# Reciprocals of attention's column sums moved from ScalarE to VectorE, in a transformer layer on eight cores

## The reference, cut to what matters

```python
# x: (8, 2048, 1024) float32; 16 heads of 64
def attn(x, W_qkv, W_out):
    qkv = einsum('bsd,ndh->bnsh', x, W_qkv)
    q, k, v = split(qkv, 3, axis=-1)
    a = einsum('bnqh,bnkh->bnqk', q, k) / sqrt(64)
    a = softmax(a + causal_mask, axis=-1)
    out = einsum('bnqk,bnkh->bnqh', a, v)
    out = out.reshape(B, -1, S)                      # (8, 1024, 2048)
    return einsum('bds,nhd->bsd', out, W_out)        # out[b,d,s] * sum over n,h of W_out[n,h,d]

x = x + attn(layernorm(x), W_qkv, W_out)
x = x + (relu(layernorm(x) @ w1 + b1) @ w2 + b2)     # 1024 -> 4096 -> 1024
```

## Time and profile before

| what | value |
|---|---|
| median of 3 runs | 1007.05 us (1004.82 to 1007.62) |
| the profiled execution's own time | 1006.95 us |
| its span on the slowest core (core 1) | 1005.2 us |
| spans of the eight cores | 998.5 to 1005.2 us |
| PE busy | 913.5 us, 91% of the span |
| DVE busy | 426.4 us, 42% |
| ACT busy | 388.2 us, 39% |
| POOL busy | 68.0 us, 7% |

### The profile page before, as it was taken

One profiled execution on the slowest core, in us unless ns is written; L12 is line 12 of the kernel. 1 busy time (PEld: TensorE's weight loads), 2 busy tenths in 40 slices (PEclk: granted clock), 3 DMA queues, 4 the chain that ended last, 5 costly groups with the idle time before them and its releaser, 6 DMA issues.

```text
span 1005.2 us, 12813 instructions; the slowest of 8 cores (998.5 to 1005.2 us)
## 1 busy us (share of the span) xinstructions
PE 913.5 (91%) x4624; PEld 381.0 (38%) x4624; DVE 426.4 (42%) x612; ACT 388.2 (39%) x505; POOL 68.0 (7%) x54
## 2 busy tenths in 40 slices
PE   3768999998999999999672999999999999999998
PEld 1323433333333333333221444444444444444443
DVE  4662035545454646363537662037310752124301
ACT  2223369797979787888881010001000010000000
POOL 1310010101010000000003030003000020000000
PEclk9788999999999999999895999999999999999999
DMA  9930259896978000010604242023410332024111
GB/s 212 257 58 0 43 91 109 99 117 79 115 76 113 2 1 1 1 43 1 209 16 153 101 150 105 32 74 126 168 41 33 136 126 105 34 71 162 48 42 42
DMA packets 27804, 85.31 MB, mean 85 GB/s; under 512 B 2272, under 2 KB 10464, under 8 KB 22880
## 3 DMA queue, kind: packets, MB, share of 16 engines
q0 software_dynamic: 15504, 25.76, 20.1%
q1 hardware_dynamic: 12240, 58.74, 16.6%
HBM read 101.34 MB, written 25.17 MB: 126 GB/s over the span
## 4 chain that ended last, share of the span: by engine, by line
PE 81%; ACT 6%; DVE 4%; DVEq 3%; issue 3%; DMA 2%; ACTq 1%; SPq 0%
PE arena L422 22%; PE arena L444 22%; PE arena L345 11%; PE arena L308 9%; PE arena L325 8%; PE arena L287 5%; ACT p_sb L520 4%; PE arena L334 2%; DMA x_sb<-x 2%; DVEq L549 2%; PE arenab L268 1%; DVE osc_sb L569 1%; ACT lnf_sb L466 1%; DVE t_sb L585 1%; ACTq L511 1%
## 5 line engine op out<-in xcount | busy, mean ns | idle before, releaser
L520 ACT ACTIVATE p_sb<-arena 128x1024 bf16<-128x1024 f32 (+1 forms) x320 | 273.4, 895 | 43.3 <-PE arena L334 26.1
L422 PE MATMUL arena<-lnf_sb,wstage 128*128 128x512 bf16 x1024 | 226.4, 382 | 1.4 <-ACT lnf_sb L466 1.4
L345 PE MATMUL arena<-p_sb,v_all 128*128 128x512 bf16 (+3 forms) x640 | 172.9, 352 | 14.2 <-DVE osc_sb L569 14.1
L422 PEld LDWEIGHTS arena<-lnf_sb,wstage 128*128 128x128 bf16 x1024 | 100.2, 98 | 121.5 <-issue 5.2
L308 PE MATMUL arena<-lnf_sb,wstage 128*128 128x512 bf16 x448 | 138.0, 380 | 0.0
L645 DVE TENSOR_SCALAR h_sb<-arena,b1c_sb 128x512 bf16<-128x512 f32 x128 | 94.9, 747 | 95.6 <-PE arena L422 95.6
L325 PE MATMUL arena<-qpair,kpair 64*128 64x512 bf16 (+3 forms) x640 | 115.3, 355 | 14.4 <-ACT p_sb L520 14.3
L444 PE MATMUL arena<-w2hi_sb,h_sb 128*128 128x512 bf16 x512 | 115.7, 379 | 0.0
L444 PE MATMUL arena<-lnf_sb,h_sb 128*128 128x512 bf16 x512 | 115.7, 379 | 0.0
L660 DVE TENSOR_TENSOR x_sb<-arena,x_sb 128x512 f32<-128x512 f32 x32 | 22.1, 692 | 198.6 <-PE arena L444 198.6
L454 ACT ACTIVATE rsd_sb<-bag_sb,cst_sb 128x2 f32<-128x2 f32 (+1 forms) x12 | 3.6, 298 | 219.2 <-DVE bag_sb L543 219.1
(11 more groups left out here) (39 smaller groups left out, 428.7 us busy)
## 6 DMA issues: line engine op xcount, KB each, us to landing
wstage<-w1b SPq DMA_DIRECT2D x32, 1024.0 KB, 4.8
x_sb<-x SPq DMA_DIRECT2D x16, 512.0 KB, 22.3
w1b<-w POOLq DMA_DIRECT2D x8, 1024.0 KB, 32.1
w2b<-w POOLq DMA_DIRECT2D x8, 1024.0 KB, 38.7
y<-x_sb SPq DMA_DIRECT2D x32, 256.0 KB, 2.0
lnf_sb<-w2b SPq DMA_DIRECT2D x2, 2048.0 KB, 16.3
w2hi_sb<-w2b SPq DMA_DIRECT2D x2, 2048.0 KB, 12.8
wstage<-wqk POOLq DMA_DIRECT2D x7, 512.0 KB, 7.9
```

What stands on the lines that cost most here:

```text
L345: mm = e.matmul(AP(arena, (4 + h) * 512 + off, [[AR, 128], [1, w]]), v_all[:, j, pair, 64 * h:64 * h + 128], AP(p_sb, (n % 3) * 1024 + h * ...
L422: mm = e.matmul(bankap(ww % 4, TF), AP(wstage, 4 * ((n // 4) % 2) * 1024 + dc * 512 + (ww % 4) * 128, [[8 * 1024, 128], [1, 128]]), lnf2_s ...
L520: e.activation(AP(p_sb, (n % 3) * 1024, [[3 * 1024, 128], [512, 2], [1, w]]), AP(arena, 2 * (n % 2) * 512 + off, [[AR, 128], [512, 2], [1, ...
```

## The change: what it does

ACT's `reciprocal` and its semaphore `act_rec` go. `o_finish` on DVE, at the same place in DVE's order, no longer waits for a semaphore. It first drains, then transposes the sums within blocks of 32 x 32 into `rec_sb`, 64 partitions for each head with the same crossing of the halves. All rows of a block of sums are equal, so after the transpose each column of a block holds its 32 different sums, and column 0 of each of the 16 blocks is enough: a new tile `r16_sb` of 128 x 16 takes the reciprocals of these 16 columns. It is multiplied by WB's 16 columns in place, and a third transpose, which reads each of the 16 columns 32 times, writes `rec_sb` in the layout of before. The four products, the sum and everything else are unchanged.

```diff
@@ tiles and semaphores
         rec_sb = asb("rec_sb", [128, 512], F32)
+        r16_sb = asb("r16_sb", [128, 16], F32)
-        act_p, act_rec = sem("act_p"), sem("act_rec")
+        act_p = sem("act_p")
@@ scalar (ACT)
-            def reciprocal(ep):
-                e.wait_ge(dve_oc, 2 * ep + 2)
-                if ep >= 1:
-                    e.wait_ge(dve_t, ep)
-                e.activation(rec_sb[0:64, :], osc_sb[64:128, ep % 2, 0:512], AF.Ln)
-                e.activation(rec_sb[64:128, :], osc_sb[0:64, ep % 2, 512:1024], AF.Ln)
-                e.drain()
-                e.activation(rec_sb[:, :], rec_sb[:, :], AF.Exp, scale=-1.0).then_inc(act_rec)
-
-            ep = 0
...
-                if n >= 3 and is_last(n - 3):
-                    reciprocal(ep)
-                    ep += 1
-            reciprocal(ep)
@@ vector (DVE), o_finish
-                e.wait_ge(act_rec, ep + 1)
+                e.drain()
+                e.transpose(rec_sb[0:64, :], osc_sb[64:128, ep % 2, 0:512])
+                e.transpose(rec_sb[64:128, :], osc_sb[0:64, ep % 2, 512:1024])
+                e.drain()
+                e.reciprocal(r16_sb[:, :], AP(rec_sb, 0, [[512, 128], [32, 16]]))
+                e.drain()
                 e.tensor_mul(
-                    AP(rec_sb, 0, [[512, 128], [32, 16], [1, 32]]),
-                    AP(rec_sb, 0, [[512, 128], [32, 16], [1, 32]]),
-                    AP(WBp_sb, pair * HD + 16 * qb, [[NPAIR * HD, 128], [1, 16], [0, 32]]))
+                    r16_sb[:, :], r16_sb[:, :],
+                    AP(WBp_sb, pair * HD + 16 * qb, [[NPAIR * HD, 128], [1, 16]]))
+                e.drain()
+                e.transpose(rec_sb[:, :], AP(r16_sb, 0, [[16, 128], [1, 16], [0, 32]]))
                 e.drain()
```

## The result

The changed kernel takes 1024.48 us at the median against 1007.34 us of the kernel before; the ratio is 1.0173, with a 95% interval from 1.0150 to 1.0195. The forecast was 1022 us, and slower. The profiled execution took 1025.08 us.

A forecast was written before the change was run, and what follows sets the result against it. PE (TensorE, 81% of the chain) was taken as the bound, stalled once a pair by VectorE's late copy; +10.9 + 8.1 - 1.0 - 2.9 - 0.1 = +15.0 us on 1006.95 gives 1022 us, range 1010 to 1034.

The forecast's parts named there:

- Work added on VectorE: In o_finish, transposes, small operations and drains ahead of the products: 2.81 us where 0.77 us stood before.
- P: Time from the start of o_finish's first instruction to its t_sb products: 0.77 us before, 2.81 us forecast, ends 1.97 and 4.64.
- the lower end of 0.41 us: Lower bound for one 512-column fp32 transpose, half of a one-source operation's 0.81 us on 1024 columns.
- rivals 3 and 4: Quick transposes (P = 1.97), 1007 to 1015 us, chance 0.11; ScalarE's relief wins (P under 1.59), 1003 us, chance 0.06.
- The stall: PE's wait for the copy at the end of block 0 grows from 1.36 to 3.17 us; six pairs, +10.9 us.
- The clock: After each of six 3.17 us PE stalls the granted clock falls, costing 1.35 us each: +8.1 us.
- Rival 1: Late copies at block 0, but the clock kept: +6.9 us, 1013.9 us, chance 0.13.
- ScalarE in pairs 1 to 6: PE's wait of 0.17 us after each of the six block 0 boundaries, following a reciprocal, goes: -1.0 us.
- ScalarE in pair 7: PE's waits of 1.34 us at blocks 1 to 2 and 2 to 3 go, exponentials start 1.46 us earlier: -2.9 us.
- Pair 7's first stall: Pair 6's finish reaches its products at 482.67 instead of 482.78: -0.1 us; the 3.81 us stall and slow clock stay.
- The tail: At the end of attention, the last products start at 528.60 against 528.61: nothing.

The follow-up runs named there:

- e5: Kernel before, with 1.83 us of unused added work on VectorE in the finish of query block 3 only; 1024.5 and 1028.3 us, ratio 1.0191.
- e6: Kernel before, with the same 1.83 us of added VectorE work in the finishes of blocks 0, 1 and 2 only; 1009.5 us.
- e3: Changed kernel with twelve extra matmuls, their sums overwritten, in each of six places where PE waits for the late copy; 1015.0 us, ratio 1.0077.
- e10: Changed kernel with every output copy ahead of the competing finish on VectorE (finishes after steps 3, 11, 23, 27); 987.0 us, ratio 0.9803.
- e11: Kernel before, reciprocals on ScalarE with two buffers, all copies first (finishes after steps 3, 11, 23, 27); 990.96 us, ratio 0.9842.
- e7: Changed kernel with transposes, reciprocal and WB product moved to right behind the output copy, ahead of the next eviction; 1010.23 us, ratio 1.0034.
- e4: Changed kernel with the copy ahead of the finish at the end of block 0 only; 1038.33 us, ratio 1.0303.
- e2: Kernel before, copies ahead of finishes at blocks 0 and 1, later finishes moved, two reciprocal buffers; 991.37 us, ratio 0.9844.

## Why the prediction was right, step by step

Measured between the profiled executions on core 1, where the end of the last copy's wait moved by 543.01 - 524.34 = 18.67 us.

- *Work added on VectorE.* P was put at 2.81 us and is 2.86: transposes 0.71 us each for 0.69 taken, the small operations 0.25 and 0.17 for 0.21 each. That a one-source operation on fp32 ran at twice the rate in the earlier trace rows said nothing of the transpose, so the lower end of 0.41 us, on which rivals 3 and 4 rested, was not there. The Vector Engine (DVE) Microarchitecture Reference of the Trainium skill, section 3.8, has one element per cycle per lane. The 0.71 us agree with it, as they lie above the 0.53 us that the prediction estimated from that page.
- *The stall.* Forecast 3.17 us and +10.9 us. Measured 3.18 to 3.22 us, together 19.15 against 8.17: +11.0 us. e5 and e6 show that nearly all of the loss comes from the finishes of block 3.
- *The clock.* Forecast +8.1 us, as six times 1.35. This is the term that was mis-sized. Take the time from one stall's end to the next in the changed kernel, subtract the same of before and what stall and ScalarE changed: -0.1, 2.5, 1.4, 2.6, 1.4 and 2.6 us, 10.5 in all. Five of six stalls lost the clock, and three of the slow stretches were 6.8 us long. I took 3.5 us from the earlier trace rows for all, although pair 7's own stretch in the trace of before is 6.8 us long, as this window of the kernel before lets one work out (2 x 0.34 x 10 = 6.8):

```profile
484.00:494.00 10.00, 6.56 (x28) 1.81 (x29) 7.15 (x12) 6.05 (x9) 0.00 (x0) 0.66 0.97 316
```

The rate of loss was right: 43% of 3.4 us is 1.5, and 43% of the 5.9 us of a long stretch that fall after the stall is 2.5. What was wrong is the length, and that every stall would lose the clock. The two partly cancel, one kept against three long, and that they do is luck. e3 gives 9.5 us for the same term by the measured time. Rival 1, the clock kept, was wrong.
- *ScalarE in pairs 1 to 6.* Forecast -1.0 us, measured -1.6. One of the six waits was 0.46 us and not 0.17, and in pair 6 a wait of 0.52 us near 460 us became 0.24. Both stand at the same steps on all eight cores of the kernel before, and on none of the changed kernel; what held ScalarE there was not followed.
- *ScalarE in pair 7.* Forecast -2.9 us; from the stall's end to the last copy it is -2.4 (34.48 us for 36.90). The two waits of 1.34 us went; a new one of 0.26 us before the last steps came.
- *Pair 7's first stall.* Forecast -0.1 us for the copy, measured +0.3, seen from the end of pair 6's copy (6.53 for 6.23 us): the addition at 506.49 starts 0.45 us late, with nothing shown that it waited for. It does so on all eight cores (0.44 to 0.45 us) and in e3 (0.42 to 0.43), and on none in the kernel before and in e10, so it isn't chance. What held it is open; no run was made for it. The stall itself, 4.48 for 3.81 us, looks worse than it is, as PE came 0.4 us earlier to it.
- *The tail* from the last copy to the products is 4.29 us for 4.27: nothing, as forecast.
- The rest of the 18.67 us, 0.9 us, stands before the attention's first steps (PE's wait near 135 us comes at 136.15 for 135.23), where the code is the same in both kernels.

The sum of the shown terms is 11.0 + 10.5 - 1.6 - 2.4 + 0.3 = +17.8 us for +15.0 forecast and +17.1 measured at the median. So the mechanism was right at each step, and the size of the clock term is what the forecast was short of.

## What to carry to other kernels

Ask of work moved to an engine with spare time not how busy that engine is, but what stands behind the work in its order and who waits for that: here 8 places of 32 cost nearly everything, and putting the copies first turned a loss of 17 us into a gain of 20, of which the kernel before gets 16 by the order alone (e11). A stall of the matmul engine has a second price in the clock: in this kernel up to 1.4 us for one of 1.9 us, and up to 2.6 for one of 3.2. So a stall that a change makes longer should be priced at both. Judge a move between engines only in the best order of each: the change is +17 us in the old order and -4 us in the new.

## What the runs showed of the hardware

- A VectorE transpose within 32x32 blocks takes 0.71 us for 512 fp32 columns, on 64 or 128 partitions, also across the halves and from a source read with a step of 0. The reciprocal of 16 columns takes 0.25 us.
- The granted clock around a PE stall between dense matmuls, in pairs 1 to 6 of one core each: kept at 1.4 us (six of six, kernel before), lost at 1.9 us in four of six (e7), at 3.2 us in five of six (changed kernel), at 4.7 us in six of six (e4). Over all eight cores of the same traces: none of 48 lost at 1.4 us, 35 of 48 at 1.9, 39 of 48 at 3.2, all 48 at 4.3 to 4.8. The length doesn't decide alone: in e5 stalls of 3.1 to 3.4 us lost it in 28 of 48. The slow stretch was 3.4 or 6.8 us and nothing between: always 3.4 in e7, always 6.8 in e4, both in the changed kernel. A slow stretch of 6.8 us cost 2.5 to 2.6 us, one of 3.4 us 1.4.
- A fall of the clock can also go with short waits close together: in pair 7 of e2, PE waited 0.75, 0.46, 0.30 and 0.85 us within 6 us, and the clock fell for 3.4 us at the last of them, which the 0.72 in this window of e2 shows; in e11 nearly the same four waits kept it.

```profile
472.00:478.00 6.00, 5.15 (x22) 1.25 (x20) 4.82 (x8) 5.71 (x8) 0.00 (x0) 0.72 0.97 362
```

- Twelve useless matmuls in a stall paid for themselves (9.5 us in six places, e3).
